# Self attention: who scales x in the layer norm

## The reference

```
def _layernorm(x, axis=-1, eps=1e-05):
    m = jnp.mean(x, axis=axis, keepdims=True)
    v = jnp.var(x, axis=axis, keepdims=True)
    return (x - m) / jnp.sqrt(v + eps)
...
    x = x + attn(_layernorm(x))      # 16 heads of 32, causal softmax, biases, output projection
    x = x + xattn(_layernorm(x))     # 16 heads of 128 on 64 context tokens
    x = x + ffn(_layernorm(x))       # 8 experts of rank 64, the best one per token
```

## Time and profile before

| | |
|---|---|
| Runs | 1561.12, 1558.29 and 1561.13 us, median 1561.12 |
| The profiled execution | 1559.77 us, of which 1557.7 is the span of the profile |
| TensorE matmul busy | 1413.5 us, 91% |
| VectorE busy | 1098.9 us, 71% |
| ScalarE busy | 729.7 us, 47% |
| GpSimd busy | 756.1 us, 49% |
| TensorE's mean granted clock | 0.962 of full |

### The profile page before, as it was taken

One profiled execution on the slowest core, in us unless ns is written; L12 is line 12 of the kernel. 1 busy time (PEld: TensorE's weight loads), 2 busy tenths in 40 slices (PEclk: granted clock), 3 DMA queues, 4 the chain that ended last, 5 costly groups with the idle time before them and its releaser, 6 DMA issues. The chain is left out here.

```text
span 1557.7 us, 28131 instructions
## 1 busy us (share of the span) xinstructions
PE 1413.5 (91%) x10464; PEld 1152.7 (74%) x10464; DVE 1098.9 (71%) x2065; ACT 729.7 (47%) x1736; POOL 756.1 (49%) x573
## 2 busy tenths in 40 slices
PE   7886889999999999999996479999999999999998
PEld 5665667777777878777775358887878788878886
DVE  4345486877777787868764577878787878787864
ACT  5444466776676767666774232323222323232321
POOL 2321266767676776767676342423333333333310
PEclk9999889999999999999997689999999999999999
DMA  9998487888898978797888442212030303030000
GB/s 324 304 330 274 102 147 141 159 166 169 152 176 162 165 160 165 150 164 156 157 159 185 159 169 74 82 60 103 26 131 27 135 27 128 27 135 27 28 14 28
DMA packets 378998, 212.16 MB, mean 136 GB/s; under 512 B 337792, under 2 KB 337920, under 8 KB 375168
## 3 DMA queue, kind: packets, MB, share of 16 engines
q1 hardware_dynamic: 378880, 210.63, 55.7%
HBM read 76.37 MB, written 50.33 MB: 81 GB/s over the span
## 5 line engine op out<-in xcount | busy, mean ns | idle before, releaser
L623 POOL TENSOR_TENSOR shared<-a_probs,shared 128x768 f16<-128x768 f32 (+1 forms) x192 | 349.6, 1821 | 190.4 <-DVE shared L794 172.4
L692 ACT ACTIVATE a_probs<-a_score,a_neg_max 128x128 f32<-128x128 f32 (+3 forms) x512 | 264.6, 530 | 201.3 <-DVE a_neg_max L785 173.8
L785 DVE TENSOR_REDUCE a_neg_max<-a_score 128x2 f32<-128x256 f32 (+3 forms) x256 | 203.5, 816 | 108.5 <-PE a_score L911 107.9
L1185 POOL TENSOR_TENSOR b_probs<-b_probs,b_row_scale 128x1024 f32<-128x1024 f32 x32 | 61.2, 1911 | 176.1 <-DVE b_row_scale L1386 176.1
L937 PE MATMUL a_out_y<-a_v,a_turned 128*128 128x96 bf16 x1280 | 123.7, 212 | 19.2 <-DMA a_turned<-shared 11.1
L937 PEld LDWEIGHTS a_out_y<-a_v,a_turned 128*128 128x128 f16 x1280 | 99.7, 100 | 53.5 <-issue 36.5
L1155 POOL TENSOR_TENSOR b_rstd<-b_var,b_minus_half 128x1 f32<-128x1 f32 x64 | 35.1, 549 | 198.9 <-DVE b_var L1307 198.8
L1259 ACT ACTIVATE b_probs<-b_probs 128x1024 f32<-128x1024 f32 x32 | 33.9, 1060 | 197.2 <-DVE b_probs L1378 197.2
L938 PE MATMUL a_out_y<-a_v,a_turned 128*128 128x64 bf16 x1280 | 119.5, 197 | 0.0
L44 PE MATMUL a_gemm<-a_xt_hi,w_self_hi 128*128 128x512 f32 x256 | 112.1, 438 | 6.3 <-DVE a_yt_lo L759 4.5
L44 PE MATMUL b_score<-b_m_hi,b_xt_hi 128*128 128x512 f32 x256 | 105.4, 412 | 12.7 <-DVE b_m_lo L1342 9.0
(11 more groups left out here) (184 smaller groups left out, 3959.0 us busy)
## 6 DMA issues: line engine op xcount, KB each, us to landing
m_dram<-c_m_out SPq DMA_DIRECT2D x8, 2048.0 KB, 13.7
vw_dram<-shared SPq DMA_DIRECT2D x32, 512.0 KB, 8.3
shared<-m_dram SPq DMA_DIRECT2D x8, 2048.0 KB, 7.8
b_vw_raw<-vw_dram SPq DMA_DIRECT2D x8, 2048.0 KB, 7.9
c_w_raw<-w_group_dram SPq DMA_DIRECT2D x7, 1280.0 KB, 11.4
a_x_res<-x_dram SPq DMA_DIRECT2D x32, 256.0 KB, 3.5
x_dram<-a_x_res SPq DMA_DIRECT2D x32, 256.0 KB, 2.9
b_x<-x_dram SPq DMA_DIRECT2D x32, 256.0 KB, 2.7
```

The costliest lines, as they stand in the source:

```text
L623: nc.gpsimd.tensor_tensor(part(u, 1), probs[:, u % PROB_SLOTS, 0:2 * columns_of(u // 2)], part(u, 0), ALU.subtract).then_inc(parts_ready, 1)
L692: ins = nc.scalar.activation(probs[:, u % PROB_SLOTS, to:to + width], score[:, j, at:at + width], ACT.Exp, bias=neg_max[:, c:c + 1], accum ...
L785: ins = nc.vector.tensor_reduce(neg_max[:, c:c + 2], score[:, 2 * half:2 * half + 2, at:at + width], AX, ALU.max, negate=True)
L1185: nc.gpsimd.tensor_tensor(probs[:, :, :], probs[:, :, :], row_scale[:, :].unsqueeze(2).to_broadcast([P, XH, S]), ALU.mult).then_inc(probs_ ...
```

## The change

ScalarE computes r * x + (-m * r) as an activation with a scale and a bias per row, in place of VectorE's (x - m) * r. VectorE makes the bias, `shift`, for all four tiles with one small instruction. It stands at the head of VectorE's round 6 and waits for GpSimd's power. The two scalings per round stand at the end of ScalarE's rounds 6 and 7.

```
--- before.py
+++ after.py
@@ -464,6 +464,7 @@
         beat = sb("beat", [P, TT], F32)
         var_eps = sb("var_eps", [P, TT], F32)
         rstd = sb("rstd", [P, TT], F32)
+        shift = sb("shift", [P, TT], F32)
 
         xt_hi, xt_lo = (sb(f"xt_{n}", [P, KT, T], F32R) for n in ("hi", "lo"))
         yt_hi, yt_lo = (sb(f"yt_{n}", [P, QUADS, T], F32R) for n in ("hi", "lo"))
@@ -490,7 +491,7 @@
         small_loaded, consts_pool, consts_ready = sem("small_loaded"), sem("consts_pool"), sem("consts_ready")
         x_loaded, x_res_loaded = ([sem(f"{n}{t}_loaded") for t in range(TT)] for n in ("x", "x_res"))
         x_res_ready = sem("x_res_ready")
-        var_ready, rstd_ready, xn_ready = sem("var_ready"), sem("rstd_ready"), sem("xn_ready")
+        var_ready, rstd_ready, shift_ready, xn_ready = sem("var_ready"), sem("rstd_ready"), sem("shift_ready"), sem("xn_ready")
         gemm_full, gemm_drained = sem("gemm_full"), sem("gemm_drained")
         xt_hi_ready = sem("xt_hi_ready")
         qk_hi_ready = sem("qk_hi_ready")
@@ -700,6 +701,11 @@
                     act.wait_ge(turned_landed[(u - PART_SLOTS) % TURN_SLOTS], landed(u - PART_SLOTS))
                 nc.scalar.activation(part(u, 0), probs[:, u % PROB_SLOTS, 0:2 * columns_of(u // 2)], ACT.Copy).then_inc(hi_by_act, 1)
 
+            def normalise(b, t):
+                act.wait_ge(shift_ready, b)
+                nc.scalar.activation(xn[:, t, :], xn[:, t, :], ACT.Identity, bias=shift[:, t:t + 1],
+                                     scale=rstd[:, t:t + 1]).then_inc(xn_ready, 1)
+
             for use in AHEAD:
                 if use[1:] == ("qk", 0):
                     act.wait_ge(consts_ready, 3)
@@ -721,6 +727,10 @@
                 for use in FILLED[2 * r - 2] + FILLED[2 * r - 1] if r else []:
                     if use[1] == "v":
                         values_second(use)
+                b, at = divmod(r, NR)
+                if b + 1 < B and at in (6, 7):
+                    normalise(b + 1, 2 * (at - 6))
+                    normalise(b + 1, 2 * (at - 6) + 1)
             for use in LAST[:2]:
                 high_part(use)
 
@@ -743,10 +753,10 @@
                 dve.wait_ge(moments_ready, 2 * TT * b)
                 nc.vector.tensor_scalar(var_eps[:, :], moments[:, :, 1], EPS, None, ALU.add).then_inc(var_ready, 1)
 
-            def ln_normalise(b, t):
+            def ln_shift(b):
                 dve.wait_ge(rstd_ready, b)
-                nc.vector.tensor_scalar(xn[:, t, :], xn[:, t, :], moments[:, t, 0:1], rstd[:, t:t + 1],
-                                        ALU.subtract, ALU.mult).then_inc(xn_ready, 1)
+                nc.vector.scalar_tensor_tensor(shift[:, :], moments[:, :, 0], -1.0, rstd[:, :],
+                                               ALU.mult, ALU.mult).then_inc(shift_ready, 1)
 
             def low_part(use):
                 b, kind, n = use
@@ -815,6 +825,8 @@
             dve.wait_ge(vw_stored, XG * 64 + 64)
             for r in range(B * NR):
                 b, at = divmod(r, NR)
+                if b + 1 < B and at == TT + 2:
+                    ln_shift(b + 1)
                 row_max(2 * r)
                 if is_round(r - BEHIND - 1):
                     outputs(r - BEHIND - 1)
@@ -832,9 +844,6 @@
                         ln_moments(b + 1, at - 2)
                     if at == TT + 1:
                         ln_variance(b + 1)
-                    if at in (6, 7):
-                        ln_normalise(b + 1, 2 * (at - 6))
-                        ln_normalise(b + 1, 2 * (at - 6) + 1)
             for use in late(2 * B * NR - 1):
                 low_part(use)
             parts_hi(2 * B * NR - 1)
```

## The result

| | before | after |
|---|---|---|
| median of 12 runs each, us | 1557.99 (1552.74 to 1561.13) | 1565.76 (1559.83 to 1571.58) |
| ratio of the runs, 95% interval | 1 | 1.0057 (1.004 to 1.0073) |
| the profiled execution: its time and its span, us | 1559.77, 1557.7 | 1566.94, 1565.1 |
| VectorE busy, us | 1098.9 | 1074.3 |
| ScalarE busy, us | 729.7 | 750.5 |

The change makes the kernel 0.57% slower, 8.9 us by this ratio; the two medians lie 7.8 us apart. The forecast was 1571, or 10.7 us more than the profiled execution before.

A forecast was written before the change was run, and what follows sets the result against it. The prediction took TensorE's waits in self attention, chiefly round 6's for yt's low part, as the bound. Delay 6.3, batch 0 2.9 and clock 1.5 sum to 10.7 us over 1559.8: 1571, own range 1566 to 1576, 8 in 10 1560 to 1577.

The forecast's parts named there:

- What bounds: Self attention: TensorE's stream sets the time; in round 6 the output product waits 2.37 us for VectorE's low part of yt.
- The delay, 2.55 us: Head of VectorE's round 6, batches 1 to 6: the shift makes the maxima start 2.55 us later.
- The handshake: Head of VectorE's round 6: waiting for GpSimd's power alone delays what is queued behind by 1.4 us.
- the blocking: Shift beside GpSimd's bias addition: it waits until 300.33, raising the delay from 1.4 to 2.55 us; rival without it, 0.17.
- One GpSimd operation or two: Forecast: the shift waits for one GpSimd operation; rival: for both, maxima 4.65 us late, time 1585, chance 0.06.
- What is swallowed, 1.5 us a batch: VectorE's cast in round 6: its existing stall absorbs 1.5 us, leaving 1.05 a batch, 6.3 in six; rival, nothing swallowed: 0.05.
- Batch 0, 2.9 us: Batch 0: the shift waits for `parts_lo`, the next `parts_lo` comes 3.0 later, and TensorE loses about 2.9 us.
- The clock, 1.5 us with a bound of 3.0: TensorE after round 6's stalls: clock falls in five batches, not four, 1.5 us more; bounds -6.0 to +3.0.
- ScalarE costs nothing: ScalarE's rounds 6 and 7: scalings of 0.70 us, 1.4 a round, fit in idle time; cost 0, bound 20 us.
- the cover of 0.7: ScalarE in round 6: scaling until 308.1, needed free at 308.8, leaving 0.7 us to spare.
- VectorE's relief counts for nothing: Removing 28.3 us of VectorE scalings, rounds 6 and 7, gains nothing; rival that it counts: 1557, chance 0.05.
- The sum: Whole kernel: 6.3 + 2.9 + 1.5 = 10.7 us more than the profiled 1559.8, forecast as 1571.

The follow-up runs named there:

- the shift late: Changed kernel with the shift moved from the head of VectorE's round 6 to its end, scalings still on ScalarE: 1556.88 us, ratio 0.9997.
- clearing the cast from the path: Kernel before the change, with yt's low part made ahead of the long cast in VectorE's round 6: 1542.18 us, ratio 0.9904; again 1543.69, 0.9922.
- the handshake kernel: Changed kernel with the shift at the end of round 6, but VectorE still waiting for GpSimd's power at its head: 1552.53 us, ratio 0.9982.
- the bias addition first: Changed kernel with GpSimd's bias addition ahead of its power, so that `parts_lo` follows the power in every batch: 1581.22 us, ratio 1.0152.
- the second profile: The changed kernel, unaltered, run and profiled once more: 1565.55 us, ratio 1.0068.
- a cleared round 6: Changed kernel with the shift at the end of round 6 and yt's low part ahead of the cast: 1537.58 us, 0.9866; again 1538.27, 0.9881.
- 30 dense matmuls: Kernel before the change, with 30 dummy matmuls into the output product's own bank, which ran behind the stall: 1570.32 us, ratio 1.0096.
- A filled stall: Kernel before the change, with 32 dummy matmuls into unused columns of another bank, ahead of the output product's first wait: 1548.62 us, ratio 0.9951.

## Why the prediction was right, step by step

- **What bounds.** Right: TensorE's waits in round 6 decide. Taking the shift out of its place removes the loss (the shift late, 0.9997), and clearing the cast from the path gains 1%.
- **The delay, 2.55 us.** Measured 2.38 (2.46 less the 0.08 of before). The handshake was priced at 1.4 and is 1.2: the maxima of the handshake kernel start at +1.30. The other 1.2 us are the blocking. Both rows it was judged by the earlier trace rows were of other operations, and the four-column shift behaves as they do: 1.24 us beside the addition, 2.08 beside `parts_lo`, 0.15 beside nothing. The prediction says that both rows agree with the rule for two SBUF inputs; only the one at 974.45 is such an instruction, while the scaling at 878.71 reads one tensor and two values per row. The Trainium skill's rule (page "SBUF — State Buffer", section "Who interferes with whom"), that of two such instructions the later is blocked for the whole of the other, agrees with the shift: it ends 0.02 us behind GpSimd's operation in the changed kernel, with the bias addition first and with the shift late.
- **One GpSimd operation or two.** Right: one. The shift ends 0.02 us behind the addition, and `parts_lo` runs beside the maxima.
- **What is swallowed, 1.5 us a batch.** Right: the cast fell to 0.68 us, and yt's low part is late by 0.88 (forecast 1.05): 5.3 us in six batches against 6.3. The stalls of 1.87 and 1.25 were forecast as 2.1 and 1.3.
- **Batch 0, 2.9 us.** The shift took 2.08 us there (forecast: about 2.2). From its variance to the next the batch is 85.79 us in place of 83.64, 2.15 more; in the second profile 1.1 more. Too large by 0.8 to 1.8. The next `parts_lo` starts 7.07 us behind the variance (216.27 and 209.20), before 4.08 (218.24 and 214.16): 3.0 later, as forecast. But TensorE, which waits for the DMA that turns its result, goes on at 222.91, 13.71 us behind the variance, and 11.80 before: 1.9 later. The DMA landed 4.5 us behind this `parts_lo`'s end and had taken 5.35 before; the forecast took it as fixed.
- **The clock, 1.5 us with a bound of 3.0.** This is the mis-sized term. Before, a fall cost 1.5 us, in four batches (6.0 us) or, in the shift-late kernel with the same single stall, in five (7.5). After, the batch lengths are 22.64, 21.74, 21.62, 22.99, 22.26 and 21.75, against 19.35 + 0.88 = 20.23 without a fall: 11.6 us, in the second profile 8.6. A fall no longer costs 1.5 but 1.4 to 2.8 (0.37 to 2.5 in the second profile): in batches 1, 4 and 5 it stands at half for 6.8 us in place of 3.4, and in batch 1 it is there before the output product restarts, so that the whole stretch behind runs slow, where in the earlier trace rows only a part of it did. Why the falls are longer behind two stalls no run here shows. So +5.6 by the first pair of traces, +1.1 to +2.6 by the second profile. The bound assumed that only the number of falls can change, not their length.
- **ScalarE costs nothing.** Right in the result: there is no wait for the scaled xn on TensorE. A scaling takes 0.83 us, not 0.70, and a pair 1.52 to 1.56 us from start to end, not 1.4, which uses up 0.12 to 0.16 us of the cover of 0.7. Round 7's first exponentials still wait 3.01 us for maxima, part of it because TensorE's slow stretch ahead makes these late.
- **VectorE's relief counts for nothing.** Right here, and not a rule: behind a cleared round 6 the kernel with it is about 5 us faster, of which 1.3 to 3.2 us lie in self attention.
- **The sum.** 5.3 + 2.15 + 5.6 = 13.1 us; self attention, from its first score to yt's last transpose, is 688.4 us before and 701.6 after, 13.2 more. The second profile has 697.5, 9.1 more. The first profiled execution is only 7.4 us longer in its span, mainly since the code ahead of self attention, the same in both, happened to take 5.2 us less (first score at 170.57, before at 175.75). Over the runs the difference is 8.9 us, inside what the steps give with the smaller clock term: 5.3 + 1.1 to 2.15 + 1.1 to 2.6 = 7.5 to 10.1. That the forecast's 10.7 came near is in part luck: it had the swallowed delay too large by 1.0 us and batch 0 by 0.8 to 1.8, and the clock too small by up to 4.1. The median, 1565.76, lies just below the forecast's own range (1566 to 1576) and inside the one of 8 in 10 (1560 to 1577); of the 5.2 us to the forecast, 1.8 come from its base, the profiled execution, which took 1559.77 where the median of twelve is 1557.99.

## What to carry to other kernels

A small instruction at the head of an engine's queue costs what everything behind it loses: here four columns, waiting for another engine and then for that engine's next operation, cost 0.57%, and at the end of the same round nothing. Before offloading work to relieve an engine, clear what stands ahead of the critical instruction in its queue; here that order gave 0.8 to 1.0%, and only then was the offloaded kernel faster, by another 0.4%. Where TensorE must stall, count the stall and the slow stretch behind it as two costs, and let the second vary with where the stalls lie.

## What the runs showed of the hardware that I had not expected

- A VectorE scalar_tensor_tensor of 128x4 with two SBUF inputs took 0.15 us alone and 1.24 or 2.08 us beside a GpSimd operation of 1.28 or 2.12 us; even a tensor_scalar of 128x4 with one input took 0.84 us beside one (0.17 elsewhere).
- Idle total alone does not tell whether TensorE's clock falls: stalls of 0.73 + 1.52 us dropped it in two batches of six, one of 2.37 in four or five, and in one when 30 dense matmuls followed it, 1.87 + 1.25 in five or six. A filled stall dropped it in none, and gave back 7.6 us without moving a single result.
- The code ahead of self attention took between 169.73 and 178.03 us in profiled executions of kernels that share it, as much as the change itself costs; a single pair of spans can't price a change of this size.
